# Gate and up by seven block products instead of eight, in a mixture of experts on one Trainium2 core

## The reference

```python
# x: 16 sequences x 256 tokens x D=256; E=8 routed experts and a shared one, F=1024
g = jnp.einsum('bsd,edf->ebsf', h, Wg)
u = jnp.einsum('bsd,edf->ebsf', h, Wu)
expert_outs = jnp.einsum('ebsf,efd->ebsd', jax.nn.silu(g) * u, Wd)
expert_output = jnp.einsum('be,ebsd->bsd', gating_probs, expert_outs)
shared = jnp.einsum('bsf,fd->bsd', jax.nn.silu(h @ Sg) * (h @ Su), Sd)
out = x + (1.0 - sg) * expert_output + sg * shared
```

## Time and profile before

| | us |
|---|---|
| Median of 3 runs | 2370.45 (2370.25 to 2370.57) |
| Span of the profiled execution | 2368.9 |
| TensorE busy (10368 matmuls) | 2355.2, 99% |
| VectorE busy | 973.8, 41% |
| ScalarE busy | 757.2, 32% |
| GpSimd busy | 30.3, 1% |

### The profile page before, as it was taken

One profiled execution on the slowest core, in us unless ns is written; L12 is line 12 of the kernel. 1 busy time (PEld: TensorE's weight loads), 2 busy tenths in 40 slices (PEclk: granted clock), 3 DMA queues, 4 the chain that ended last, 5 costly groups with the idle time before them and its releaser, 6 DMA issues.

```text
span 2368.9 us, 29088 instructions
## 1 busy us (share of the span) xinstructions
PE 2355.2 (99%) x10368; PEld 1947.9 (82%) x10368; DVE 973.8 (41%) x1385; ACT 757.2 (32%) x1228; POOL 30.3 (1%) x20
## 2 busy tenths in 40 slices
PE   8999999999999999999999999999999999999999
PEld 6888888888888888888888888888888888888887
DVE  6333533344333533343333433353334433353333
ACT  3222322233222322233233323242223322232222
POOL 5000000000000000000000000000000000000000
PEclk9999999999999999999999999999999999999999
DMA  5000100000000100010000100010000100000000
GB/s 179 1 0 0 54 0 0 0 27 27 0 0 0 53 0 0 0 41 12 0 0 3 51 0 0 0 53 0 0 0 20 33 0 0 0 0 18 18 9 27
DMA packets 13183, 36.98 MB, mean 16 GB/s; under 512 B 1488, under 2 KB 1632, under 8 KB 13168
## 3 DMA queue, kind: packets, MB, share of 16 engines
q1 hardware_dynamic: 13104, 36.71, 4.7%
q0 software_dynamic: 64, 0.07, 0.1%
HBM read 32.58 MB, written 4.19 MB: 16 GB/s over the span
## 4 chain that ended last, share of the span: by engine, by line
PE 98%; DVE 1%; DMA 0%; ACT 0%; issue 0%; SPq 0%; DVEq 0%
PE down_ps L172 11%; PE up_ps L174 11%; PE up_ps L172 11%; PE up_ps L173 11%; PE down_ps L174 11%; PE down_ps L173 11%; PE gate_ps L174 11%; PE gate_ps L172 11%; PE gate_ps L173 11%; DMA acc<-xT 0%; DVE w_lo L368 0%; DVE h_lo L404 0%; DVE h L397 0%; ACT h_hi L300 0%; DVE acc L485 0%
## 5 line engine op out<-in xcount | busy, mean ns | idle before, releaser
L397 DVE TENSOR_TENSOR h<-silu,up_ps 128x512 f32<-128x512 f32 x576 | 396.0, 687 | 1067.0 <-PE up_ps L174 1066.3
L300 ACT CAST h_hi<-h 128x512 fp32r<-128x512 f32 x576 | 357.4, 621 | 872.7 <-DVE h L397 872.7
L294 ACT ACTIVATE silu<-gate_ps 128x512 f32<-128x512 f32 x576 | 344.5, 598 | 724.3 <-PE gate_ps L174 724.1
L404 DVE TENSOR_TENSOR h_lo<-h,h_hi 128x512 fp32r<-128x512 f32 x576 | 407.7, 708 | 311.8 <-ACT h_hi L300 303.2
L172 PE MATMUL down_ps<-h_hi,w_hi 128*128 128x512 f32 x1152 | 448.7, 390 | 1.0 <-DVE h_lo L404 0.8
L172 PE MATMUL up_ps<-x_hi,w_hi 128*128 (+1 forms) x1152 | 448.6, 389 | 0.0
L173 PE MATMUL up_ps<-x_lo,w_hi 128*128 (+1 forms) x1152 | 448.6, 389 | 0.0
L174 PE MATMUL up_ps<-x_hi,w_lo 128*128 (+1 forms) x1152 | 448.6, 389 | 0.0
L173 PE MATMUL down_ps<-h_lo,w_hi 128*128 128x512 f32 x1152 | 448.2, 389 | 0.0
L174 PE MATMUL down_ps<-h_hi,w_lo 128*128 128x512 f32 x1152 | 448.2, 389 | 0.0
L172 PE MATMUL gate_ps<-x_hi,w_hi 128*128 (+1 forms) x1150 | 447.6, 389 | 0.0
(11 more groups left out here) (31 smaller groups left out, 281.9 us busy)
## 6 DMA issues: line engine op xcount, KB each, us to landing
w_raw<-w SPq DMA_DIRECT2D x71, 384.0 KB, 3.0
acc<-xT SPq DMA_DIRECT2D x7, 512.0 KB, 11.7
outT<-acc SPq DMA_DIRECT2D x7, 512.0 KB, 2.6
acc<-xT SPq DMA_DIRECT2D x2, 256.0 KB, 5.5
outT<-acc SPq DMA_DIRECT2D x2, 256.0 KB, 2.0
w_raw<-w SPq DMA_DIRECT2D x1, 256.0 KB, 8.3
w_raw<-w SPq DMA_DIRECT2D x1, 128.0 KB, 2.7
probs_sb<-probs POOLq DMA_DIRECT2D x1, 64.0 KB, 5.7
```

Of the source, the lines that this page charges most:

```text
L294: nc.scalar.activation(silu[:, k % S_BUFS, :], gate_ps[:, k % 2, :], ACT.Silu).then_inc(silu_done, 1)
L300: nc.scalar.copy(h_hi[:, k % H_BUFS, :], h[:, k % S_BUFS, :]).then_inc(h_hi_done, 1)
L397: nc.vector.tensor_tensor(h[:, k % S_BUFS, :], silu[:, k % S_BUFS, :], up_ps[:, k % 2, :], ALU.mult).then_inc(prod_done, 1)
L404: nc.vector.tensor_tensor(h_lo[:, k % H_BUFS, :], h[:, k % S_BUFS, :], h_hi[:, k % H_BUFS, :].bitcast(F32), ALU.subtract).then_inc(h_split, 1)
```

## The change

For a pair of tiles (0 and 1) and a chunk, gate and up are one product of 2 x 2 blocks: blocks of weights A (gate and up by two feature halves) times blocks of tokens B (two feature halves by two tiles). Before, these were eight block products. Now they are seven, of sums and differences of blocks:

- P1 = A11\*B11, P2 = A12\*B21, P5 = S1\*T1, P6 = S2\*T2, P3 = S4\*B22, P7 = S3\*T3, P4 = A22\*T4
- S1..S4 are four weight blocks, T1..T4 four token blocks, each made of sums and differences.
- gate of tile 0 = P1 + P2; the other three outputs are longer sums. A PSUM bank collects P1, then P6, P7 and P4; another P5, then P3. In between ScalarE reads the running sum out ("taps"): `tap_p1` after P1, `tap_u2` after P6, `tap_p5` after P5. VectorE adds the taps to the banks: `gate` of tile 0 and 1, `up1`.

The token pairs are now the outermost loop (4 groups), the experts within. So the weights of a chunk are loaded, summed and split again for each pair, 288 times in place of 72, through a ring of four slots. GpSimd makes the four sums of 128 columns (L168) and the `lo` part of nine blocks, in three instructions of 384 columns (L183); ScalarE the `hi` part, 1152 columns (L323). The coefficient goes into `h` (L410 for tile 0, L422 for tile 1, two halves of 256 columns each), so that the down sums of all experts and chunks of a group stay in PSUM and are added to `acc` once per group (L456). The token forms of the next group are made by GpSimd and ScalarE while the first expert of a group runs, those of the first group by VectorE. On TensorE a unit (group, expert, chunk) is P1, P5, P2, P6, down of tile 1, P3, P7, down of tile 0, P4; the two downs are those of the unit before.

Cut to its core (weight sums and `lo` parts and the head of the loop on GpSimd, whose wait for token tiles 2 and 3 is L239; the unit on TensorE; `h` of tile 1 on VectorE):

```diff
+            def weight_sums(n, s):
...
+                step(S1, A21, A22, ALU.add)
+                step(S3, A11, A21, ALU.subtract)
+                pool.wait_ge(w_sums, 4 * n + 1)
+                step(S2, S1, A11, ALU.subtract)
+                pool.wait_ge(w_sums, 4 * n + 3)
+                step(S4, A12, S2, ALU.subtract)
+            def weight_lo(n, s):
+                pool.wait_ge(w_hi_done, n + 1)
+                for part in range(3):
+                    c = cols(3 * part, 3 * part + 2)
+                    ins = nc.gpsimd.tensor_tensor(
+                        w_lo[:, s, c], w_raw[:, s, c], w_hi[:, s, c].bitcast(F32), ALU.subtract
+                    )
+                ins.then_inc(w_lo_done, 1)
...
+                if g + 1 < GROUPS:
+                    pool.wait_ge(pair_loaded[g], 32)
+                for k in range(CHUNKS):
+                    steady(0, k, new_x=g + 1 < GROUPS)
...
-            def gate_up(e, T, k, x, wait_banks=True, only_up=False):
...
+            def unit(g, e, k, first=False):
...
+                pe.wait_ge(w_lo_done, n + 1)
+                after(pe, h0_done, n - 1)
+                product(chain, s, A11, *x(B11), start=True, stop=True).then_inc(p1_done, 1)
+                after(pe, gate1_done, n)
+                product(p53_ps[:], s, S1, *x(T1), start=True, stop=True).then_inc(p5_done, 1)
+                after(pe, gate0_done, n)
+                product(p2_ps[:], s, A12, *x(B21), start=True, stop=True).then_inc(p2_done, 1)
+                pe.wait_ge(p1_tapped, n + 1)
+                product(chain, s, S2, *x(T2), start=False, stop=True, goes_on=True).then_inc(p6_done, 1)
...
+                pe.wait_ge(up1_done, n + 1)
+                product(chain, s, A22, *x(T4), start=False, stop=True, goes_on=True).then_inc(p4_done, 1)
...
-                nc.vector.tensor_tensor(
-                    h[:, k % S_BUFS, :], silu[:, k % S_BUFS, :], up_ps[:, k % 2, :], ALU.mult
-                ).then_inc(prod_done, 1)
+            def h1(g, e, n):
+                dve.wait_ge(silu_done[1], n + 1)
+                dve.wait_ge(up1_done, n + 1)
+                after(dve, h_lo_done[1], n)
+                for half in range(HALVES):
+                    s = half_of(half)
+                    ins = nc.vector.scalar_tensor_tensor(
+                        h[:, 1, s], silu[:, 1, s], coef_of(g, e, 1, half), up1[:, s], ALU.mult, ALU.mult
+                    )
+                ins.then_inc(h1_done, 1)
```

More of the change, by code:

```diff
@@ L64, in moe_kernel @@
         acc = sb("acc", [P, TILES, DC, TOKENS])
[L65 to L73, removed]
+        x_sum = sb("x_sum", [P, 4, TOKENS])
+        x_hi = sb("x_hi", [P, 2, X_FORMS, TOKENS], F32R)
+        x_lo = sb("x_lo", [P, 2, X_FORMS, TOKENS], F32R)
+        w_raw = sb("w_raw", [P, SLOTS, FORMS * P])
+        w_hi = sb("w_hi", [P, SLOTS, FORMS * P], F32R)
+        w_lo = sb("w_lo", [P, SLOTS, FORMS * P], F32R)
+        tap_p1 = sb("tap_p1", [P, TOKENS])
+        tap_p5 = sb("tap_p5", [P, TOKENS])
+        tap_u2 = sb("tap_u2", [P, TOKENS])
+        gate = sb("gate", [P, 2, TOKENS])
+        up1 = sb("up1", [P, TOKENS])
+        silu = sb("silu", [P, 2, TOKENS])
+        h = sb("h", [P, 2, TOKENS])
+        h_hi = sb("h_hi", [P, 2, TOKENS], F32R)
+        h_lo = sb("h_lo", [P, 2, TOKENS], F32R)
         probs_sb = sb("probs_sb", [P, BATCH, ROUTED])
@@ L109, in moe_kernel @@
+        h1_done = sem("h1_done")
+        h_lo_done = [sem(f"h{t}_lo_done") for t in range(2)]
+        added = [sem(f"added{t}") for t in range(2)]
         coef_steps = sem("coef_steps")
@@ L113, in moe_kernel, with after @@
         block = ctx.enter_context(nc.Block())
+        def after(engine, signal, count):
+            if not isinstance(count, int) or count > 0:
+                engine.wait_ge(signal, count)
         @block.sync
@@ L168, in _ @@
         @block.tensor
         def _(pe):
[L170 to L183, removed]
@@ L216, in down, with product @@
[L216 to L221, removed]
+            def product(bank, s, form, hi, lo, start, stop, goes_on=False):
+                c = slice(form * P, (form + 1) * P)
+                on = dict(skip_group_check=goes_on)
+                nc.tensor.matmul(bank, w_hi[:, s, c], hi, start=start, stop=False, **on)
+                nc.tensor.matmul(bank, w_hi[:, s, c], lo, start=False, stop=False, **on)
+                return nc.tensor.matmul(bank, w_lo[:, s, c], hi, start=False, stop=stop, **on)
@@ L275, in _ @@
+            for g in range(GROUPS):
+                for k in range(CHUNKS):
+                    unit(g, 0, k, first=(k == 0))
+                with pe.Fori(1, EXPERTS) as e:
+                    for k in range(CHUNKS):
+                        unit(g, e, k)
+            for t in (1, 0):
+                pe.wait_ge(h_lo_done[t], LAST + 1)
+                down(GROUPS - 1, CHUNKS - 1, t, start=False, stop=True)
         @block.scalar
         def _(act):
-            def split_weights(e, k, down_unit=None):
-                act.wait_ge(w_loaded[k], (e + 1) * 16)
-                if down_unit is not None:
-                    act.wait_ge(down_done, down_unit + 1)
-                nc.scalar.copy(w_hi[:, k, :], w_raw[:, k, :]).then_inc(w_hi_done, 1)
@@ new lines, in h_hi_of, with unit @@
+            def h_hi_of(t, n, done):
+                act.wait_ge(done, n + 1)
+                after(act, down_done[t], n)
+                nc.scalar.copy(h_hi[:, t], h[:, t]).then_inc(h_hi_done[t], 1)
+            def unit(g, e, k, new_x=False):
+                n = g * PER + e * CHUNKS + k
+                first = isinstance(n, int) and n == 0
+                act.wait_ge(p1_done, n + 1)
+                after(act, gate0_done, n)
+                nc.scalar.copy(tap_p1[:], chain_ps[:, k % 2, :]).then_inc(p1_tapped, 1)
+                act.wait_ge(p5_done, n + 1)
+                after(act, up1_done, n)
+                nc.scalar.copy(tap_p5[:], p53_ps[:]).then_inc(p5_tapped, 1)
+                if not first:
+                    h_hi_of(0, n - 1, h0_done)
+                act.wait_ge(p6_done, n + 1)
+                after(act, gate1_done, n)
+                nc.scalar.copy(tap_u2[:], chain_ps[:, k % 2, :]).then_inc(u2_tapped, 1)
+                act.wait_ge(gate0_done, n + 1)
+                after(act, h0_done, n)
+                nc.scalar.activation(silu[:, 0], gate[:, 0], ACT.Silu).then_inc(silu_done[0], 1)
+                if not isinstance(n, int) or n + AHEAD <= LAST:
+                    weight_hi(n + AHEAD, (k + AHEAD) % SLOTS)
+                if new_x:
+                    for form in X_AT.get(k, ()):
+                        x_form_hi(g + 1, form)
+                act.wait_ge(gate1_done, n + 1)
+                after(act, h1_done, n)
+                nc.scalar.activation(silu[:, 1], gate[:, 1], ACT.Silu).then_inc(silu_done[1], 1)
+                h_hi_of(1, n, h1_done)
@@ L350, in _ @@
[L350 to L359 removed]
+            x_form_hi(0, B11)
@@ new lines, in _ @@
+            weight_hi(0, 0)
+            for form in range(1, X_FORMS):
+                x_form_hi(0, form)
+            weight_hi(1, 1)
+            for g in range(GROUPS):
+                for k in range(CHUNKS):
+                    unit(g, 0, k, new_x=g + 1 < GROUPS)
+                last_group = g == GROUPS - 1
+                with act.Fori(1, EXPERTS - 1 if last_group else EXPERTS) as e:
+                    for k in range(CHUNKS):
+                        unit(g, e, k)
+                if last_group:
+                    for k in range(CHUNKS):
+                        unit(g, EXPERTS - 1, k)
@@ L408, in tile @@
-            def tile(T, parity, previous=None, first=False, splits=None):
-                for k in range(CHUNKS):
-                    between = None
-                    if previous is not None and 1 <= k <= HALVES:
-                        def between(half=k - 1):
-                            add_tile(T - 1, previous, 1 - parity, half)
-                    unit(T, k, first, between)
-                    if splits is not None:
-                        splits(k)
-            def first_splits(k):
-                if k + LEAD < CHUNKS:
-                    split_weights(0, k + LEAD)
@@ new lines, in h1, with h_lo_of @@
+            def h1(g, e, n):
+                dve.wait_ge(silu_done[1], n + 1)
+                dve.wait_ge(up1_done, n + 1)
+                after(dve, h_lo_done[1], n)
+                for half in range(HALVES):
+                    s = half_of(half)
+                    ins = nc.vector.scalar_tensor_tensor(
+                        h[:, 1, s], silu[:, 1, s], coef_of(g, e, 1, half), up1[:, s], ALU.mult, ALU.mult
+                    )
+                ins.then_inc(h1_done, 1)
+            def h_lo_of(t, n):
+                dve.wait_ge(h_hi_done[t], n + 1)
+                after(dve, down_done[t], n)
+                nc.vector.tensor_tensor(h_lo[:, t], h[:, t], h_hi[:, t].bitcast(F32), ALU.subtract).then_inc(
+                    h_lo_done[t], 1
```

(55 more changed lines are left out.)

466 lines of the change are left out of this document (207 added, 259 removed).

## The result

2306.16 us, median of 4 runs (2303.67 to 2307.02), against 2370.35 before (median of 4 runs here); the ratio is 0.9728 (95% interval 0.9714 to 0.9741), 64 us less. Forecast: 2286, range 2188 to 2380. The profiled execution spans 2305.0 us.

The account below looks back on a forecast made before the run. It took TensorE as the bound, busy 2355.2 of 2368.9 us. Start 21, matmuls 2154.5, blocked units 95, group ends 9 and end 5 gave 2284.5 us of span, 2286 of time; range 2188 to 2380.

Parts of the forecast that it names:

- TensorE's work: On TensorE, 9504 matmuls at 0.2267 us each, 2154.5 us in all; 7.48 us per unit of 33.
- The blocking: VectorE's two-SBUF-input instructions and GpSimd's SBUF reads exclude each other; h1 is delayed, making a unit 0.36 us too long.
- What a blocked instruction saves: Once let in, a blocked VectorE instruction costs its length less 0.15 us, a blocked GpSimd one less 0.12.
- piece 3: GpSimd's third w_lo instruction of 384 columns in a unit, forecast to run between the halves of h1, ending at 6.33 us.
- The fixed part of a GpSimd instruction: Column-independent cost of GpSimd's short instructions, taken as 0.15 us, giving 0.99 us for 384 columns and 0.43 for 128.
- The second rival: Short GpSimd instructions are dear: fixed cost above 0.25 us, 2336 us at 0.25, slower than before from 0.32; chance 0.22.
- VectorE asks first: Rival: h1's halves go ahead of GpSimd's second and third w_lo instructions, or are not blocked; 2191 us, chance 0.28.
- The margin of 0.26 us: In a unit, GpSimd's second w_lo instruction begins 0.26 us before h1 can start, so h1's first half waits.
- The count of units: The 0.36 us delay holds in about 265 of 288 units, 95 us; first ten and eight behind each group end excepted.
- The sum: Whole kernel: 2284.5 us of span, 2286 of time, 84 us faster than before.
- start: Before the first product: waits for weights, sums, w_hi, w_lo and token tiles 2 and 3, 21 us.
- three group ends, 3 us each, and the units behind them free: At each group end two adds of 1024 columns stand ahead of h0 on VectorE, 3 us each, 9 in all.

Follow-up runs that it names:

- e4: Changed kernel with h1 as one VectorE instruction of 512 columns instead of two halves, the second sequence's coefficient left out: 2194.1 us.
- e1: Changed kernel with GpSimd's w_lo of a unit made in nine instructions of 128 columns instead of three of 384: 2206.2 us.
- e5: Changed kernel with w_hi on ScalarE moved ahead of silu of tile 0, so GpSimd's w_lo instructions start earlier: 2213.1 us.
- e6: Changed kernel with w_hi on ScalarE moved behind silu of tile 1, so GpSimd's w_lo instructions start later: 2199.8 us.
- e7_start: Changed kernel with GpSimd's wait for token tiles 2 and 3 (L239) moved a unit later: 2303.9 us.
- e3: Changed kernel with tap_p1 of a unit put ahead of h_hi1 of the unit before on ScalarE: 2268.9 us.

## Why the prediction was right

- *TensorE's work.* 9504 x 0.2267 us: e4 and e1 run whole experts at 7.48 per unit. Right.
- *The blocking* was right in kind and size, and it does reach scalar_tensor_tensor, which no row of before had shown: 476 ns undisturbed, 1114 in the median. `h0`, with one input in PSUM, took 469 ns in the mean beside a busy GpSimd. The Trainium skill ("SBUF — State Buffer", section "Who interferes with whom") says both, and the trace agrees. What a blocked instruction saves was read a little off: the earlier trace rows give 0.15 and 0.13 us for GpSimd, not 0.12, and in the unit above piece 3 saves 0.11 and the first half of `h1` 0.20, not 0.15. Of this 0.05 a half the unit shows little, as `h1` also began 0.08 us late.
- *The fixed part of a GpSimd instruction.* Taken as 0.15. From 0.989 at 384 columns and 0.443 at 128 it is 0.17, and 2.13 ns a column. The second rival (over 0.25) falls.
- *VectorE asks first* (0.28) did not happen here, but e4, e5, e1 and e6 each brought its time about, 2194 to 2213 for 2191. The margin of 0.26 us by which piece 2 came first was 0.29 (`h1` at 4.51; piece 2 began at 311.44, which is 4.22).
- *The count of units* was wrong by its own list: the first ten and three times eight leave 254 of 288, not 265, and 254 x 0.36 is 91 us, not 95. A unit was 0.376 too long, not 0.36, and the two errors made up for each other: that this term came out within 1 us is in part luck.
- *The sum* was 20.5 us short (2284.5 of span against 2305.0). From the starts of `tap_p1`, 288 in all:

| term | forecast | measured |
|---|---|---|
| start | 21 | 20.1 |
| TensorE's matmuls | 2154.5 | 2154.5 |
| units of experts 2 to 9: too long | 95 | 95.9 (255 x 0.376) |
| first experts and group ends | 9 | 27 |
| end | 5 | 7.7 |

The term that was mis-sized is "three group ends, 3 us each, and the units behind them free". The three ends cost 4.7, 4.3 and 2.0. At each `h0` waits for two adds (2.34 us, priced at 2.5). At the first two, `h_lo` of tile 1 then comes 0.06 us behind a token form of 512 columns on GpSimd and takes 1.75 us (timelines of VectorE and GpSimd at the first group end):

```profile
596.75 2.34 DVE L456 TENSOR_TENSOR acc<-down_ps,acc 128x1024 f32<-128x1024 f32 x2
...
599.01 0.86 DVE L410 SCALAR_TENSOR_TENSOR h<-silu,coef,chain_ps 128x256 f32<-128x256 f32 x2
599.79 1.75 DVE L430 TENSOR_TENSOR h_lo<-h,h_hi 128x512 fp32r<-128x512 f32 x1
```

```profile
599.73 1.26 POOL L200 TENSOR_TENSOR x_sum<-acc,x_sum 128x512 f32<-128x512 f32 x1
```

So TensorE waits 2.60 us for it, and behind that wait its clock falls (view by stretches: stretch, its length, busy us of PE, PEld, DVE, ACT and POOL, granted clock, DMA share, GB/s; then a matmul in it and the next):

```profile
603.00:606.00 3.00, 3.00 (x9) 2.32 (x8) 0.69 (x1) 1.88 (x3) 2.08 (x3) 0.50 0.00 0
```

```profile
603.24 0.63 PE L256 MATMUL p_ps<-x_hi,w_hi 128*128 128x512 f32 x1
603.67 0.63 PE L257 MATMUL p_ps<-x_lo,w_hi 128*128 128x512 f32 x1
```

The granted clock is 0.50, the lower level (1.2 GHz), and eight matmuls start 0.43 us apart instead of 0.23: 1.6 us. The second end shows the same, at 1173 us. The prediction had neither the block nor the clock in this term. At the third end no token forms are left to make; `h_lo` takes 0.68, TensorE waits 1.55 us, and the clock stays full:

```profile
1739.32 0.68 DVE L430 TENSOR_TENSOR h_lo<-h,h_hi 128x512 fp32r<-128x512 f32 x1
```

The clock does not follow the length of the wait alone: in e7_start, with the same three waits, it is full behind the first and 0.50 behind the second and the third. What decides it, no run shows.

The first two units lost some 6 us. About half of it is slow matmuls, 0.43 us apart from 20.65 to 25.77, behind 20 us in which TensorE did nothing:

```profile
20.65 0.63 PE L257 MATMUL chain_ps<-x_lo,w_hi 128*128 128x512 f32 x1
21.08 0.63 PE L258 MATMUL chain_ps<-x_hi,w_lo 128*128 128x512 f32 x1
```

The profile gives the granted clock as 1.00 here; that it was the lower level I conclude from the distance, which is that of 603 us. The rest are waits, 1.1 us for `up1` and 1.7 for the second `tap_p1`.

The other units of first experts lost 10 us together, which I have not taken apart; I had set them to nothing because their phase moves, and it moves both ways. At the end TensorE waits 1.57 us for the last `h_lo`, which I left out.

## What to carry to other kernels

When an idle engine gets work, look in the old trace for the few microseconds in which it did work, and at what the others' instructions lasted there: eight rows gave the time of a unit here to 0.02 us. Where two engines exclude each other for whole instructions, totals say nothing; draw the path in time, see who asks when, and either cut the long instruction (e1), take one turn instead of two (e4) or move one to where its partner has room (e6). Here each gave back about 100 us, more than the 64 that the change itself gained. And a wait of TensorE can cost more than its length: behind 2.60 us of waiting, the slower matmuls cost 1.6 us more.

## What the runs showed that I had not expected

The gain of e3: taking away the wait that all units showed (140.9 us at the weight loads) gave 37 us, since the next wait stood 0.16 us behind it. And the clock behind the first two group ends: no row of before had such a stretch at a group end to learn from. A small one: `silu` from SBUF takes 0.634 us, from PSUM 0.598; whether it is a part of the 0.08 us by which `h1` started late, no run shows.
